# A new order of the work on four engines in the attention and routing stage of a decoder layer

## The reference

```python
x = layernorm(x + dilated_attention(x))           # 16 heads of 16; segments of 64, every 2nd token
x = layernorm(x + cross_attention(x, ctx, Wq, Wkv, Wout))   # 16 heads, causal, keys/values from ctx
probs = softmax(x @ gate_w)                       # routing: 32 experts
w, sel = top_k(probs, 8); w = w / sum(w)          # 8 experts a token, at most 1024 pairs an expert
y = sum over the 8 of w * (silu(x @ w_gate[e]) * (x @ w_up[e])) @ w_down[e]
x = layernorm(x + y)
```

## Time and profile before

| | us |
|---|---|
| median of 3 runs (lowest, highest) | 600.43 (600.2, 601.47) |
| the profiled execution | 601.89 |
| its span, from the first instruction to the last | 600.1 |

### The profile page before, as it was taken

The page is one execution under the profiler, slowest core; times in us unless marked ns, Lnnn a source line. Parts: engine busy times, 40 slices in busy tenths (PEclk is TensorE's granted clock), DMA queues, the critical chain, the costliest instruction groups (busy, mean ns, idle before and its releaser), DMA issues.

```text
span 600.1 us, 16476 instructions
## 1 busy us (share of the span) xinstructions
PE 511.5 (85%) x4567; PEld 407.5 (68%) x4568; DVE 393.8 (66%) x1571; ACT 334.6 (56%) x1208; POOL 387.4 (65%) x596
## 2 busy tenths in 40 slices
PE   2789898888888888888517999999999999995894
PEld 2556555565556555554206999999999999994683
DVE  1368777877778777886343666666666666664875
ACT  2265666667665655666303666666666767671112
POOL 6542766566666766655671888888888878883433
PEclk9999999999999999999756999999999999997999
DMA  9299999997122222222234666666666666666995
GB/s 196 78 330 269 284 346 376 342 337 251 69 76 87 87 76 76 77 73 84 93 126 141 202 202 187 194 195 205 185 201 196 186 198 185 199 195 262 427 419 184
DMA packets 79835, 118.48 MB, mean 197 GB/s; under 512 B 12339, under 2 KB 69565, under 8 KB 77760
## 3 DMA queue, kind: packets, MB, share of 16 engines
q1 hardware_dynamic: 63456, 78.63, 43.6%
q0 software_dynamic: 13824, 37.78, 17.0%
q10 hardware_dynamic: 2528, 1.74, 1.0%
HBM read 56.07 MB, written 66.22 MB: 204 GB/s over the span
## 4 chain that ended last, share of the span: by engine, by line
PE 45%; POOL 16%; issue 12%; DVE 12%; DMA 7%; ACT 6%; POOLq 1%; SPq 0%; DVEq 0%; ACTq 0%
PE bank L804 17%; POOL queues L539 11%; PE bank L820 11%; PE bank L796 6%; DMA wall<-results 5%; ACT pr L900 4%; PE bank L814 3%; DVE kP L1073 3%; PE bank L618 1%; POOL rz L502 1%; PE bank L608 1%; POOL rz L496 1%; DVE nmax L1050 1%; PE bank L669 1%; DMA cs<-in_ctx 1%
## 5 line engine op out<-in xcount | busy, mean ns | idle before, releaser
L563 POOL DMA_INDIRECT results<-ys,wcol x152 | 150.5, 990 | 26.0 <-POOL pscrap L552 23.8
L539 POOL DMA_INDIRECT queues<-x,xidx x128 | 128.2, 1002 | 37.0 <-issue 37.0
L804 PE MATMUL bank<-wall,xtT 128*128 x624 | 129.3, 330 | 0.0
L900 ACT ACTIVATE pr<-bank,nmax 128x128 f32<-128x128 f32 x256 | 90.9, 371 | 28.1 <-DVE nmax L1050 28.1
L804 PEld LDWEIGHTS bank<-wall,xtT 128*128 128x128 f32 x624 | 99.4, 193 | 0.1
L820 PE MATMUL bank<-wall,hT 96*128 x304 | 90.7, 379 | 0.0
L991 ACT ACTIVATE ys<-bank,wcol 128x256 f32<-128x256 f32 x152 | 72.1, 474 | 27.8 <-PE bank L820 27.8
L1261 DVE SCALAR_TENSOR_TENSOR tg<-th,bank 128x96 f32<-128x96 f32 x156 | 39.6, 254 | 58.2 <-ACT th L985 58.2
L796 PEld LDWEIGHTS bank<-ident,xt 128*128 128x128 f32 x314 | 61.7, 197 | 20.5 <-DMA xt<-queues 12.7
L796 PE MATMUL bank<-ident,xt 128*128 128x128 f32 x314 | 63.0, 281 | 12.0 <-DMA xt<-queues 12.0
L608 PE MATMUL bank<-kP,qS 128*128 128x512 f32 x128 | 66.2, 599 | 0.0
(11 more groups left out here) (189 smaller groups left out, 890.8 us busy)
## 6 DMA issues: line engine op xcount, KB each, us to landing
xt<-queues SPq DMA_DIRECT2D x162, 160.0 KB
results<-zeros SPq DMA_DIRECT2D x16, 1024.0 KB
wall<-results SPq DMA_DIRECT2D x16, 1024.0 KB, 19.8
queues<-zeros SPq DMA_DIRECT2D x2, 1760.0 KB
wall<-in_L_ffn_w_gate SPq DMA_DIRECT2D x4, 768.0 KB
wall<-in_L_ffn_w_up SPq DMA_DIRECT2D x4, 768.0 KB
wall<-in_L_ffn_w_down SPq DMA_DIRECT2D x4, 768.0 KB
results<-ys,wcol POOLq DMA_INDIRECT x152, 2.9
```

The source lines that it names most:

```text
L539: pool.indirect_dma_start(xg, bass.IndirectOffsetOnAxis(ap=xidx[:, par, k:k + 1], axis=0), x2[:, par, :], None, bounds_check=last_row, oob ...
L563: pool.indirect_dma_start(yr, bass.IndirectOffsetOnAxis(ap=wcol[:, u, 1:2], axis=0), ys[:, u, :], None, bounds_check=last_y, oob_is_err=Fa ...
L804: ins = pe.matmul(bank[2 + u % 2][:, 0:2 * INTER].rearrange("p (g i) -> p g i", g=2), xtT[:, u % 2, kk, :], wall[:, bass.ds(e, GU)].rearrange(
L900: ins = act.activation(pr[:, g % 2, q, :], pS[g % 2][:, q * P:(q + 1) * P], ACT.Exp, bias=nmax[:, 4 * g + q:4 * g + q + 1], accum_out=den[ ...
```

## The change

Nothing is computed differently; instructions and the waits ahead of them change places within a step, on four engines.

- POOL: the context's copy leaves `mask_x` and becomes `context`, which in steps with a tile r stands behind the wait for xidx. `keep` comes ahead of that wait and gets a wait of its own, for x2. `root_a` comes ahead of the scatter's k = 5 instead of k = 6.
- PE: the first attention's o comes ahead of values 0, and its wait for the turned weights moves into S2, between its two matmuls; values 1 come behind T2 and the x1 transposes; keys and values come ahead of the logits.
- ACT: the third exponentials (e2) come ahead of the copy of T1; the next tile's first exponentials (e0) go behind rT and the first attention's exponential.
- DVE: the sums' inverse and rO go behind the second norm's variance; rden goes ahead of the positions' work; positions (away, fits, near) come ahead of the weights (ew, ri, x2's tail); xidx comes ahead of the maxima of the next tile's first scores (m0).

```diff
@@ signal lists
-        dveA = Steps(sem("dveA"), "gT max sub sum inv turn own scale add stats aggr")
+        dveA = Steps(sem("dveA"), "gT max sub sum turn inv own scale add stats aggr")
-        peB = Steps(sem("peB"), "T0 S2 V0 T1 S3 V1 T2 V2 T3 V3 rT y")
+        peB = Steps(sem("peB"), "T0 S2 V0 T1 S3 T2 V1 V2 T3 V3 rT y")
-        actB = Steps(sem("actB"), "e1 T0 T1 e2 T2 e3 T3 rT")
+        actB = Steps(sem("actB"), "e1 T0 e2 T1 T2 e3 T3 rT")
-        dveR = Steps(sem("dveR"), "top clamp m8 mr pickb row ew ri away fits w seen near8 near idx")
+        dveR = Steps(sem("dveR"), "top clamp m8 mr pickb row away fits seen near8 near ew ri w idx")
@@ POOL
+            def context(a, par):
                 pool.tensor_copy(ct[:, par, 0:LAT], cs[:, bass.ds(a, 1), :].rearrange("p a d -> p (a d)")
                                  ).then_inc(poolA.sem, 1)
...
                 if a is not None and not (isinstance(a, int) and a >= NB - 2):
                     mask_x(a + 2, par)
+                    if r is None:
+                        context(a + 2, par)
...
+                    if not last:
+                        pool.wait_ge(dveN.sem, dveN.at(r + 2, "x2"))
+                        keep(r, par)
                     if isinstance(r, int) and r == 0:
                         pool.wait_ge(queues_init, 16 * (INIT + 1))
                     pool.wait_ge(dveR.sem, dveR.at(r, "idx"))
-                    if not last:
-                        keep(r, par)
+                    if a is not None and not (isinstance(a, int) and a >= NB - 2):
+                        context(a + 2, par)
                     for k in range(TOPK):
                         if k == 3 and not (isinstance(r, int) and r == NB - 1):
                             root_r(r + 3)
-                        if k == 6 and not (isinstance(r, int) and r >= NB - 3):
+                        if k == 5 and not (isinstance(r, int) and r >= NB - 3):
                             root_a(r + 3)
@@ PE
-            def scores(b, g, par):
+            def scores(b, g, par, also=None):
...
+                if also is not None:
+
+                    pe.wait_ge(*also)
                 pe.matmul(pS[g % 2][:, :], qS[:, g % 2, m, :], kP[:, par, m, :, :],
...
-                    scores(b, 2, pb)
-                if a is not None:
-
-                    pe.wait_ge(dveA.sem, dveA.at(a, "turn"))
-                if b is not None:
-
-                    if there(b - 1):
-                        pe.wait_ge(dveY.sem, dveY.at(b - 1, "add"))
-                    values(b, 0, pb)
-                if a is not None:
+                    scores(b, 2, pb, None if a is None else (dveA.sem, dveA.at(a, "turn")))
+                if a is not None:
+
+                    if b is None:
+                        pe.wait_ge(dveA.sem, dveA.at(a, "turn"))
                     for j in range(PAIRS):
...
                 if b is not None:
+
+                    if there(b - 1):
+                        pe.wait_ge(dveY.sem, dveY.at(b - 1, "add"))
+                    values(b, 0, pb)
                     turn_probs(b, 1, None)
...
                     scores(b, 3, pb)
-                    values(b, 1, pb)
                     turn_probs(b, 2, (actB.sem, actB.at(b, "T0")))
+                if a is not None:
+
+                    pe.wait_ge(actA.sem, actA.at(a, "cT"))
+                    for m in range(2):
+                        pe.matmul(pC[:, m * P:(m + 1) * P], wkvT[:, m * P:(m + 1) * P], cT[:, :],
+                                  start=True, stop=True)
+                    pe.matmul(pC[:, D:2 * D], cT[:, :], wkvT[:, D:2 * D], start=True, stop=True
+                              ).then_inc(peA.sem, 1)
                 if r is not None:
                     if a is not None:
                         pe.wait_ge(dveA.sem, dveA.at(a, "scale"))
...
                 if b is not None:
+                    values(b, 1, pb)
                     values(b, 2, pb)
@@ ACT
                     exps(b, 1)
                     probs_T(b, 0)
+                    exps(b, 2)
                     probs_T(b, 1)
-                    exps(b, 2)
...
-                if a is not None:
-                    exps(a, 0)
                 if b is not None:
                     act.wait_ge(peB.sem, peB.at(b, "rT"))
                     act.copy(flat2(rT[:, :, :]), pO[:, D:2 * D]).then_inc(actB.sem, 1)
                 if a is not None and not (isinstance(a, int) and a == NB - 1):
                     exps_A(a + 1)
+                if a is not None:
+                    exps(a, 0)
@@ DVE
                     dve.tensor_reduce(dA[:, :], eA[:, :, :], AX_X, ALU.add).then_inc(s, 1)
-                    dve.wait_ge(s, A("sum"))
-                    dve.reciprocal(rA[:, :], dA[:, :]).then_inc(s, 1)
                     dve.transpose(eAT[:, :, :, :], eA[:, :, :].unsqueeze(2).to_broadcast([P, PAIRS, DIL, GR])).then_inc(s, 1)
-                    dve.wait_ge(s, A("inv"))
-                    dve.tensor_tensor(rO[:, :, :], rA[:, :].unsqueeze(2).to_broadcast([P, PAIRS, DIL]),
-                                      own[:, ::HD].rearrange("p (j s) -> p j s", s=DIL), ALU.mult).then_inc(s, 1)
                 if r is not None:
...
                     variance(1, 2).then_inc(dveN.sem, 1)
+                if a is not None:
+                    dve.wait_ge(s, A("sum"))
+                    dve.reciprocal(rA[:, :], dA[:, :]).then_inc(s, 1)
+                    dve.wait_ge(s, A("inv"))
+                    dve.tensor_tensor(rO[:, :, :], rA[:, :].unsqueeze(2).to_broadcast([P, PAIRS, DIL]),
+                                      own[:, ::HD].rearrange("p (j s) -> p j s", s=DIL), ALU.mult).then_inc(s, 1)
...
-                    dve.wait_ge(actR.sem, actR.at(r, "e"))
-                    dve.scalar_tensor_tensor(ew[:, :], er[:, :], 1.0, pickb[:, :], ALU.mult, ALU.mult,
-                                             accum_out=es[:, :]).then_inc(t, 1)
-                    dve.wait_ge(t, R("ew"))
-                    dve.reciprocal(ri[:, :], es[:, :]).then_inc(t, 1)
+                if b is not None:
+                    dve.wait_ge(actB.sem, actB.at(b, "e3"))
+                    dve.reciprocal(rden[:, :], den[:, :]).then_inc(v, 1)
                 if r is not None:
                     dve.wait_ge(peR.sem, peR.at(r, "pos"))
...
                     dve.wait_ge(t, R("fits"))
-                    dve.scalar_tensor_tensor(x2[:, par, D:D + NE],
-                                             ew[:, :], ri[:, 0:1], fits[:, :], ALU.mult, ALU.mult).then_inc(t, 1)
-                    dve.tensor_tensor(seen[:, :], seen[:, :], pickb[:, :], ALU.add).then_inc(t, 1)
...
                     dve.max(near[:, :], away[:, :]).then_inc(t, 1)
+                    dve.wait_ge(actR.sem, actR.at(r, "e"))
+                    dve.scalar_tensor_tensor(ew[:, :], er[:, :], 1.0, pickb[:, :], ALU.mult, ALU.mult,
+                                             accum_out=es[:, :]).then_inc(t, 1)
-                if b is not None:
-                    dve.wait_ge(actB.sem, actB.at(b, "e3"))
-                    dve.reciprocal(rden[:, :], den[:, :]).then_inc(v, 1)
+                if b is not None:
                     dve.wait_ge(v, B("inv"))
                     dve.tensor_copy(rX[:, :, :], rden[:, :].unsqueeze(2).to_broadcast([P, NH, HD])).then_inc(v, 1)
+                if r is not None:
+                    dve.wait_ge(t, R("ew"))
+                    dve.reciprocal(ri[:, :], es[:, :]).then_inc(t, 1)
+                    dve.wait_ge(t, R("ri"))
+                    dve.scalar_tensor_tensor(x2[:, par, D:D + NE],
+                                             ew[:, :], ri[:, 0:1], fits[:, :], ALU.mult, ALU.mult).then_inc(t, 1)
+                    dve.tensor_scalar(xidx[:, par, :], near[:, :], -1.0, FAR, ALU.mult, ALU.add).then_inc(t, 1)
                 if a is not None:
                     maxes(a, 0)
-                if r is not None:
-
-                    dve.wait_ge(t, R("near"))
-                    dve.tensor_scalar(xidx[:, par, :], near[:, :], -1.0, FAR, ALU.mult, ALU.add).then_inc(t, 1)
```

More of the change, by code:

```diff
@@ L439, in _ @@
             mask_x(0, 0)
+            context(0, 0)
             put(pool.memset, kP[:, :, :, :, :].rearrange("p a m q k -> p (a m q k)"), 0.0)
@@ L508, in step @@
                     mask_x(1, 1)
+                    context(1, 1)
                     root_a(0)
@@ L694, in step @@
                 if a is not None:
-                    pe.wait_ge(actA.sem, actA.at(a, "cT"))
-                    for m in range(2):
-                        pe.matmul(pC[:, m * P:(m + 1) * P], wkvT[:, m * P:(m + 1) * P], cT[:, :],
-                                  start=True, stop=True)
-                    pe.matmul(pC[:, D:2 * D], cT[:, :], wkvT[:, D:2 * D], start=True, stop=True
-                              ).then_inc(peA.sem, 1)
-                if a is not None:
                     pe.wait_ge(dveN.sem, dveN.at(a, "x1"))
@@ L1169, in step @@
```

(4 more changed lines are left out.)

## The result

The changed kernel takes 573.29 us (median of four runs, 572.53 to 573.8), the kernel before 600.35 beside it (four runs, 600.2 to 601.47). The ratio is 0.9544, with a 95% interval of 0.9528 to 0.9561. The forecast was 575.0, faster. The profiled execution took 573.67, its span 571.9, and 1.8 lies outside the span, as before; so the span is 28.2 shorter.

The account below looks back on a forecast made before the run. It took a ring of waits through POOL to bound the kernel; 14 steps x (16.8 - 15.1) = 23.8, plus 2.2 at the ends, made 26 off 601.89, or 575.9; it said 575, range 564 to 590 (8 in 10).

Parts of the forecast that it names:

- M to T0: PE, from the denominators' two transposes to the first turn of probabilities: 2.75 us, waiting for the first exponentials.
- T2 to the x1 transposes: PE, from the third turn of probabilities through logits and keys/values to x1's transposes: 1.92 us, the same in either order.
- T0 to T2, all between: PE, from the first turn of probabilities to the third: 4.72 us, with none of it waiting.
- x1 transposes to S0: PE, from x1's transposes to the first scores: 3.17 us, set by ACT's chain and not touched.
- S0 to M: PE, from the first scores to the denominators' two transposes: 2.32 us.
- so I count 0: POOL's moved copies beside DVE's keys and max0: counted 0, though masked x meeting the x1 norm had cost 0.33 us.
- The new wait at T0: PE waits some 0.4 us for the first exponentials at the first turn of probabilities, replacing 1.07 for oT.
- POOL's ring: Loop through POOL's scatter DMAs and two roots and DVE's routing: 16.8 us a step before, 13.6 without waits after.
- The slower one: Rival: PE's and ACT's order sets the step; late first exponentials cost 0.4 us a step: 606 us, chance 0.06.
- It doesn't do what it says: Rival: POOL's root_r still waits for ve, losing what xidx gains: 600 us, chance 0.04.
- The larger gain: Rival: PE's waits at the first turn and first scores vanish, 14.1 us a step: 561 us, chance 0.08.
- The smaller gain: Rival: PE's lap has more waits than seen, 15.95 us a step: 588 us, chance 0.25.

Follow-up runs that it names:

- run with the exponentials in between: Changed kernel with ACT's first exponentials between rT and the attention exponential, and S2's two matmuls swapped on PE: 570.6 us, ratio 0.9492.
- the run with that edit alone: Kernel before with one edit, ACT's first exponentials behind rT and the attention exponential: 593.23 us against 601.44, ratio 0.9864.

## Why the prediction was right, point by point

**The size.** 26 was forecast as 14 steps x 1.7 and 2.2 at the ends; measured 25.5 and 2.5. The lap worked out for PE was 14.9 as a sum and 15.1 with an allowance; it is 15.02. That it comes so near is in part luck: two terms missed by more than 0.2, M to T0 too short and T2 to the x1 transposes too long, and cancel. By terms, in the step shown:

| piece | predicted | after | |
|---|---|---|---|
| M to T0 | 2.75 | 2.96 | 118.29 to 121.25 |
| T0 to T2, all between | 4.72 | 4.85 | 121.25 to 126.10 |
| T2 to the x1 transposes | 1.92 | 1.68 | 126.10 to 127.78 |
| x1 transposes to S0 | 3.17 | 3.19 | 127.78 to 130.97 |
| S0 to M | 2.32 | 2.34 | 130.97 to 133.31 |

**M to T0.** The reckoning by way of sA held in every link but one: xidx to the end of sA is 1.54 (132.83 to 134.37) for 1.5, the end of sA to T0 is 1.90 (119.35 to 121.25) for 1.96. But scan to xidx takes 1.96 for the 1.8 forecast. The scan itself is 0.17 longer. The step of the prediction that failed here is the cost that it left out, "so I count 0": the meeting of POOL's masked x is not with x1, but with the scan, which is on the lap. The mean scan is 0.47 against 0.28. What that costs can be read from the kernel with POOL's old order, where gm is over before the scan begins (scan, M, T0):

```profile
132.96 0.28 DVE L1159 TENSOR_TENSOR_SCAN x<-ones,row,pickb 128x32 int32<-128x32 f32 x1
...
135.38 0.44 PE L741 MATMUL bank<-ident,rX 128*128 128x128 f32 x2
...
138.20 0.66 PE L621 MATMUL bank<-ident,pr 128*128 128x128 f32 x4 [0.33 <-ACT pr L901]
```

The scan's start to T0 is 5.24 there and 5.41 in the changed kernel (130.87 to 136.28), M to T0 2.82 and 2.97. So the meeting costs 0.15 a step, some 2 us in 14 steps. The new wait at T0, "some 0.4", is 0.38.

**T2 to the x1 transposes** was called the same in either order and is 0.24 shorter; the run with the old order of logits and keys has a step of 14.97, and there the piece is 1.76 (126.60 to 128.36), so the order is worth 0.08 of it. The rest, 0.16, was a wait in the row that the prediction took to be free: x1 ended at 105.20 in the earlier trace rows, 0.06 ahead of the transposes, and in the kernel before their weight load waited for it in every step (85 to 272 us):

```profile
PEld bank L706 <- DVE x L1039: 3.0, 11, 0.3
```

That was POOL's ring pushing on PE's lap; with root_a earlier it is gone, and with POOL's old order in the changed kernel it is back, on PE itself. **S0** was put down to ACT's chain: the size held, but the profile names DVE's keys as what came last for PE, before and after, 0.1 or less behind ACT's scaled queries. In the run with the old order of logits and keys, where PE does not wait for the keys, the piece is 2.99 (128.36 to 131.35).

**POOL's ring** was put at 13.6 without waits and said to just fit. The run with the exponentials in between shows it: 14.91 in the eight steps from oT's fifth start on, with a wait of 0.8 a step at root_r (7.3 us in 9), so 14.1 without it, and half of these steps hold a scan that takes 0.6 more than its 0.28. root_a's place and ve coming earlier brought 1.67 of the 1.3 + 1.06: first DMA to root_a is 118.84 to 126.12, 7.28, where the earlier trace rows give 104.11 + 16.8 - 111.96 = 8.95. Of the rest, 0.30 is the wait for ve that is left at root_r; with the exponentials in between, root_r to root_a alone is 3.09 for 4.36, the 1.3 forecast for root_a's place.

**What bounded the kernel before** was half right. The ring on POOL was there, but "PE is not in it", read from the chain of the earlier trace rows, was taken for more than it says. Beside the ring lay a lap of PE, ACT and DVE, 0.14 shorter. And the chain's "issue" was not all "POOL's own gaps". In the step of the earlier trace rows it has

```profile
115.56 1.02 issue
...
116.62 0.57 POOL rz L496
```

where the timeline names ve as the end of the same wait. That is 10.0 of the 187 us, and ve follows the output projection, so at root_r the ring itself waits for PE's work. The theory built on the chain gave POOL's part alone 11 us or more, and it brought 2.2. The total did not suffer, since the new order was not priced as the old step less POOL's gains: PE's lap was laid out again, piece by piece, and the longer of the two taken. With POOL's gains alone as the sum (0.8 + 1.3 + 1.06 a step, 44 us) it would have been far off.

**The rivals.** The slower one was argued against with the same row, and that argument was worth little; what disproves it is the run with that edit alone, 8.2 us faster. "It doesn't do what it says" falls with root_r's wait, 3.8 for 10.0. The larger gain needed T0's wait away: the run that takes it away stops at 14.76, at POOL. The smaller gain, 15.95 a step, did not come; PE, counted there as busy for 14.7 of the step, is busy for 14.2.

**How much each part is worth** has no single answer. Undone in the changed kernel: the third exponentials with values 1 19.6 us, the first exponentials 9.6, POOL 5.9, values 0 4.2, max0 1.2 (0.6 by the ratios, and not told from none): about 40. Done alone in the kernel before: 2.8, 8.2 and 2.2, for the first three; the third exponentials and POOL's part together 11.0. The change is worth 27.1. Not tried alone: DVE's positions ahead of the weights, and the place of the sums' inverse.

## What to carry to other kernels

The chain that ended last names one lap; another may lie a hundredth beside it, and then either half of a change gives little alone. So price a new order by laying out every lap that closes on itself through each engine, in the new order, and take the longest. And when one engine's work is moved, look which instruction on the other engine it meets next, not only whether the old meeting is gone. A piece that the chain calls "issue" can be a wait: hold it against the rows of waits.

## What the runs showed of the hardware

Whether a DVE scan of 128x32 meets POOL's multiplication of 128x256 (gm) is decided by a few hundredths of a microsecond. In the run with the exponentials in between, two steps in a row:

```profile
129.35 0.28 DVE L1172 TENSOR_TENSOR_SCAN x<-ones,row,pickb 128x32 int32<-128x32 f32 x1
129.43 0.76 POOL L421 TENSOR_TENSOR gm<-xs,own 128x256 f32<-128x256 f32 x1
```

and the pair at 144.08 above. With 0.08 of lead the scan took 0.28, and gm no longer than elsewhere; with 0.04 of lead it took 0.88 and ended at 144.96, 0.10 behind gm's end. In the changed kernel gm led by 0.39, and the scan of 130.87 ended at 131.32, 0.09 behind gm's end. So the scan waits for the whole of a gm that came first, and a lead of 0.04 in the records is not yet first. A longer lead does not free it either. In the run with both parts together (POOL's and the third exponentials') scans began 0.35 to 0.37 ahead of gm, while POOL's last DMA instruction was still running, and took 0.51 to 0.54:

```profile
152.06 0.98 POOL L548 DMA_INDIRECT queues<-x,xidx  x1 [0.31 <-issue]
152.69 0.52 DVE L1166 TENSOR_TENSOR_SCAN x<-ones,row,pickb 128x32 int32<-128x32 f32 x1
```

This one ended at 153.21, 0.17 behind the end of that DMA instruction. That gm holds up the scan agrees with the Trainium skill ("SBUF — State Buffer", section "Who interferes with whom"): a VectorE instruction with two inputs in SBUF contends with a GpSimd instruction that reads SBUF, and the order of issue decides who blocks. The Trainium skill (the same page, section "Terms") states too that the loser of the ports that the two engines share blocks fully; the gm of 129.43, which came second, shows no such loss (0.76 for 0.74).
